# Local-attention layers: VectorE's mask and rows, ScalarE's table load, squares and copies in another order

## The reference, cut to what matters

```python
def attn_layer(x, Wqkv, qs, ksc, Wo):
    q, k, v = (sh(t) for t in jnp.split(x @ Wqkv, 3, -1))   # 16 heads of 64
    q, k = l2norm(q) * qs, l2norm(k) * ksc
    q = q * cos * scale + rotate_half(q) * sin * scale
    k = k * cos / scale + rotate_half(k) * sin / scale
    return local_attention(q, k, v) @ Wo                    # windows of 32, softmax over 64 keys

def ffn_layer(x, g, bln, W1, b1, W2, b2):
    a, gate = jnp.split(layernorm(x, g, bln) @ W1 + b1, 2, -1)
    return a * gelu(gate) @ W2 + b2

for i in range(6):
    x = attn_layer(shift_tokens(x), ...) + x
    x = ffn_layer(shift_tokens(x), ...) + x
```

## Time and profile before

| | |
|---|---|
| three runs | 2000.18, 2004.35, 2007.57 us, median 2004.35 |
| profiled execution, own time | 1996.81 us |
| its span | 1995.0 us |
| mean granted TensorE clock | 0.967 |
| first key projection of `local_layers` | 373.04 us into the span |
| end of its last step | about 1972 us |

### The profile page before, as it was taken

One profiled execution on the slowest core, in us unless ns is written; L12 is line 12 of the kernel. 1 busy time (PEld: TensorE's weight loads), 2 busy tenths in 40 slices (PEclk: granted clock), 3 DMA queues, 4 the chain that ended last, 5 costly groups with the idle time before them and its releaser, 6 DMA issues. The chain is left out here.

```text
span 1995.0 us, 59622 instructions
## 1 busy us (share of the span) xinstructions
PE 1797.9 (90%) x24192; PEld 1002.1 (50%) x24192; DVE 1538.6 (77%) x2549; ACT 1374.7 (69%) x2874; POOL 1262.5 (63%) x1127
## 2 busy tenths in 40 slices
PE   5898898679999999999999999999999999999974
PEld 3444444355555555555555555555555555555541
DVE  4778887357888888887888888888888888887833
ACT  1454445447878877787778887788877887778832
POOL 4303210248877877777777877778777787777710
PEclk8899999889999999999999999999999999999986
DMA  8000000323433333333443333333334333333300
GB/s 177 21 2 1 2 2 2 85 51 79 107 70 73 88 84 83 72 71 73 89 88 77 70 73 87 88 81 71 73 80 90 86 70 70 72 68 80 76 1 22
DMA packets 137216, 132.63 MB, mean 66 GB/s; under 512 B 79336, under 2 KB 82984, under 8 KB 136616
## 3 DMA queue, kind: packets, MB, share of 16 engines
q1 hardware_dynamic: 136944, 128.81, 29.1%
HBM read 20.94 MB, written 1.05 MB: 11 GB/s over the span
## 5 line engine op out<-in xcount | busy, mean ns | idle before, releaser
L1023 ACT ACTIVATE prob<-s_in,lower,rq 128x64 f32<-128x64 f32 x1536 | 542.9, 431 | 31.4 <-POOL lower L1193 31.1
L827 PE MATMUL bank_a<-x_shift,wqk_sb 128*128 128x512 f32 x768 | 369.4, 604 | 3.2 <-PEq L65 1.8
L1164 POOL TENSOR_TENSOR prob<-prob,rden 128x1024 f32<-128x1024 f32 x96 | 182.6, 1902 | 146.4 <-DVE rden L1244 146.3
L827 PEld LDWEIGHTS bank_a<-x_shift,wqk_sb 128*128 128x128 f32 x768 | 146.8, 195 | 183.0 <-issue 178.8
L1183 POOL TENSOR_TENSOR kfin<-rk,kfin 128x512 f32<-128x512 f32 x96 | 122.2, 1273 | 155.6 <-ACT rk L1119 107.1
L1009 ACT ACTIVATE zT<-bank_z 128x1024 f32<-128x1024 f32 x192 | 191.9, 1012 | 22.7 <-PE bank_z L838 22.7
L384 ACT ACTIVATE a_prob<-a_sT 128x1024 f32<-128x1024 f32 x128 | 130.5, 1023 | 103.5 <-PE a_sT L218 101.5
L493 DVE TENSOR_REDUCE a_negmax<-a_max 128x1 f32<-128x512 f32 x256 | 164.7, 685 | 47.8 <-PE a_max L168 44.2
L846 PE MATMUL bank_y<-zT,wvo_high 128*128 128x512 f32 x384 | 186.8, 609 | 0.9 <-ACT zT L1009 0.9
L846 PE MATMUL bank_y<-zT,wvo_low 128*128 128x512 f32 x384 | 186.1, 607 | 1.0 <-ACT zT L1009 1.0
L838 PE MATMUL bank_z<-pT,xk_prev 32*128 32x128 f32 x3072 | 167.1, 286 | 9.7 <-DVE xn L1266 5.2
(11 more groups left out here) (176 smaller groups left out, 4120.2 us busy)
## 6 DMA issues: line engine op xcount, KB each, us to landing
kpad<-kfin SPq DMA_DIRECT2D x384, 128.0 KB, 2.4
qpair<-qfin SPq DMA_DIRECT2D x384, 128.0 KB, 2.4
wqk_sb<-in_wqkv SPq DMA_DIRECT2D x40, 128.0 KB, 2.7
xk_prev<-xk_own SPq DMA_DIRECT2D x24, 192.0 KB, 2.6
ffn_sb<-in_ffn SPq DMA_DIRECT2D x6, 537.5 KB, 4.2
wvo_low<-in_wqkv SPq DMA_DIRECT2D x6, 256.0 KB, 5.7
wvo_low<-in_wo SPq DMA_DIRECT2D x3, 512.0 KB, 6.9
wvo_high<-in_wqkv SPq DMA_DIRECT2D x6, 256.0 KB, 4.8
```

What stands on the lines that cost most here:

```text
L827: last = pe.matmul(bank_a[:, half, :], wqk_sb[:, layer_of(u) % 2, part, half, g * P:(g + 1) * P], cols(u), start=True, stop=True)
L1023: last = act.activation(prob[:, n % 2, i, :], s_in[:, n % 2, i, :], ACT.Exp, bias=lower[:, n % 2, i:i + 1], scale=rq[:, n % 2, i:i + 1])
L1164: pool.tensor_tensor(prob[:, e % 2], prob[:, e % 2], rden[:].unsqueeze(2).broadcast_to([P, TPB * GH, 2 * WIN]), ALU.mult).then_inc(pn_ok, 1)
```

## The change

ScalarE, gelu step: the load of the ln and exp table stands between the key squares; ten exponentials follow it instead of nine; one more comes after the key norms; rq comes ahead of the first query square; both copies stand between the two query squares; exponentials 11 to 14 close the step, and number 15 opens the next one, under the same semaphore. ScalarE, other steps: the copy of banks 2 and 3 comes ahead of the second query square, and xnT behind exponentials 6 to 11. VectorE: mask and floor come ahead of xn; the pieces of ADD and OUTPUT stand at other places of the listing.

```diff
@@ scalar, step @@
+                if quarter(e) and unit_at(s - 1, LINEAR) is not None:
+                    exponentials(e, 15, TPB * GH).then_inc(exp_ok, 1)
                 if u_gelu is not None:
...
                         act.activation(sq[:, 0, :], bank_a[:, 0, :], ACT.Square).then_inc(sqk0_ok, 1)
+                    act.preload_act_table_set("natural_log_exp_and_others")
+                    if quarter(n):
                         after(act, pk2_ok, n)
                         act.activation(sq[:, 1, :], bank_a[:, 1, :], ACT.Square).then_inc(sqk_ok, 1)
-                    act.preload_act_table_set("natural_log_exp_and_others")
...
-                        exponentials(d, 0, 9)
+                        exponentials(d, 0, 10)
...
-                        after(act, q_mm, n)
-                        after(act, sumk_ok, n)
-                        act.activation(sq[:, 0, :], bank_a[:, 0, :], ACT.Square).then_inc(sqq0_ok, 1)
+                    if quarter(d):
+                        exponentials(d, 10, 11)
                     if quarter(c):
...
                     if quarter(n):
-                        after(act, pq2_ok, n)
-                        act.activation(sq[:, 1, :], bank_a[:, 1, :], ACT.Square).then_inc(sqq_ok, 1)
-                    if quarter(d):
-                        exponentials(d, 9, 11)
+                        after(act, q_mm, n)
+                        after(act, sumk_ok, n)
+                        act.activation(sq[:, 0, :], bank_a[:, 0, :], ACT.Square).then_inc(sqq0_ok, 1)
...
                         copy(z[:, 0:2, :], bank_z[:, 0:2, :]).then_inc(z01_ok, 1)
+                    if quarter(n):
+                        after(act, pq2_ok, n)
+                        act.activation(sq[:, 1, :], bank_a[:, 1, :], ACT.Square).then_inc(sqq_ok, 1)
                     if quarter(d):
-                        exponentials(d, 11, 16).then_inc(exp_ok, 1)
+                        exponentials(d, 11, 15)
                 else:
...
+                    if quarter(d):
+                        exponentials(d, 6, 12)
                     u_turned = unit_at(c, NORM)
...
-                    if quarter(d):
-                        exponentials(d, 6, 12)
...
-                    if quarter(n):
-                        after(act, pq2_ok, n)
-                        act.activation(sq[:, 1, :], bank_a[:, 1, :], ACT.Square).then_inc(sqq_ok, 1)
                     if quarter(e):
...
                         copy(z[:, 2:4, :], bank_z[:, 2:4, :]).then_inc(z23_ok, 1)
+                    if quarter(n):
+                        after(act, pq2_ok, n)
+                        act.activation(sq[:, 1, :], bank_a[:, 1, :], ACT.Square).then_inc(sqq_ok, 1)
@@ vector, step @@
-                if u_back is not None:
-                    after(dve, rstd_ok, u_back)
-                    after(dve, xnT_mm, u_back - 1)
-                    for t in range(TPB):
-                        last = dve.tensor_scalar(xn[:, t, :], ...)
-                    last.then_inc(xn_ok, 1)
                 if quarter(c):
...                                                    (mask)
                     dve.tensor_scalar(rk[:], bank_f[:], 1e-24, None, ALU.max).then_inc(floor_ok, 1)
+                if u_back is not None:
+                    after(dve, rstd_ok, u_back)
+                    after(dve, xnT_mm, u_back - 1)
+                    for t in range(TPB):
+                        last = dve.tensor_scalar(xn[:, t, :], ...)
+                    last.then_inc(xn_ok, 1)
+                if quarter(n):
...                                                    (query products, maxima)
+                if u_add is not None:                  (ADD, moved ahead of the folds and SUM)
+                    after(dve, y_mm, 4 * u_add + 3)
...
-                if u_add is not None:
...
+                if u_out is not None:                  (OUTPUT, moved ahead of LINEAR)
+                    after(dve, ff_mm, u_out)
...
-                if u_out is not None:
```

More of the change, by code:

```diff
@@ L1261, in step @@
                                   prob[:, e % 2].rearrange("p h (k n) -> p h k n", n=WIN)).then_inc(pT_ok, 1)
-                if u_back is not None:
-                    after(dve, rstd_ok, u_back)
-                    after(dve, xnT_mm, u_back - 1)
-                    for t in range(TPB):
-                        last = dve.tensor_scalar(xn[:, t, :], bank_z[:, 2, t * P:(t + 1) * P], mv[:, t, 0:1],
-                                                 rstd[:, t:t + 1], ALU.subtract, ALU.mult)
-                    last.then_inc(xn_ok, 1)
                 if quarter(c):
@@ L1279, in step @@
                     dve.tensor_scalar(rk[:], bank_f[:], 1e-24, None, ALU.max).then_inc(floor_ok, 1)
+                if u_back is not None:
+                    after(dve, rstd_ok, u_back)
+                    after(dve, xnT_mm, u_back - 1)
+                    for t in range(TPB):
+                        last = dve.tensor_scalar(xn[:, t, :], bank_z[:, 2, t * P:(t + 1) * P], mv[:, t, 0:1],
+                                                 rstd[:, t:t + 1], ALU.subtract, ALU.mult)
+                    last.then_inc(xn_ok, 1)
+                if quarter(n):
                     after(dve, q_mm, n)
@@ L1288, in step @@
                     dve.tensor_reduce(s_max[:], s_in[:, c % 2], AX.X, ALU.max, negate=True).then_inc(max_ok, 1)
+                if u_add is not None:
+                    after(dve, y_mm, 4 * u_add + 3)
+                    lo, hi = cols(u_add, 0, 64), cols(u_add, 64, P, 1)
+                    dve.tensor_tensor(lo, bank_y[0:64, :], lo, ALU.add)
+                    dve.tensor_tensor(hi, bank_y[64:P, :], hi, ALU.add).then_inc(xa_ok, 1)
                 if s < FOLD_STEPS:
@@ L1301, in step @@
                     last.then_inc(mv_ok, 1)
-                if u_add is not None:
[L1303 to L1306, removed]
+                if u_out is not None:
+                    after(dve, ff_mm, u_out)
+                    lo, hi = cols(u_out, 0, 64), cols(u_out, 64, P, 1)
+                    dve.scalar_tensor_tensor(lo, bank_z[0:64, 3, :], ff_column(u_out, 2 * FCH)[0:64], lo, ALU.add, ALU.add)
+                    dve.scalar_tensor_tensor(hi, bank_z[64:P, 3, :], ff_column(u_out, 2 * FCH)[64:P], hi, ALU.add,
+                                             ALU.add).then_inc(xf_ok, 1)
                 if u_lin is not None:
```

## The result

The changed kernel took 1992.75 us in the median of four runs (1990.03 to 1994.42), the kernel before 2003.21 (2000.18 to 2007.57, four runs): ratio 0.9945, interval 0.9923 to 0.9967. A second comparison, with six runs against thirteen, gave 0.9945 again (0.9924 to 0.9967). The forecast was 1993.0. That this number was met so closely is luck; it hides two errors that cancel: the steady steps gave 6 us, not 12, and 4 to 5 us net came from stalls that the forecast had not looked at.

What follows compares the result with a forecast made beforehand. TensorE was taken as the bound. Four steps of 61.88 against 62.47 us gave 0.57 a unit, 12.5 for 22, cut to 11.4 for early steps and stalls: 1993.0 from the median 2004.35, range 1984 to 2001.

Steps and rivals of the forecast that it cites:

- L838 ... must now wait ... 0.37 lost: Norm step: L838 overwrites the bank xn reads, so it waits for the later xn, costing TensorE 0.37 us.
- sumq then ends ... 2.48 into the gate step: GpSimd's queue moves forward by 0.53 us, so sumq ends 2.48 us into the gate step, against 3.15.
- The gelus at 1.29: Gelu step: ScalarE does not follow the shorter gate step, so gelus start 1.29 us in, before at 0.80.
- L940 starts at 6.91: Gelu step: the later second key square and sumk make L940 start at 6.91 us, before 6.58; cost 0.32.
- the third rival: Gelu steps: an unseen drain behind the table load delays L940 by 1.38 us each; slower, 2023 us; chance 0.02.
- The fourth: The square ahead of the last four exponentials delays exp_ok by 0.5 in three of four steps; say 2018 us; chance 0.05.
- The first: The xn wait doesn't bind and the gelu step's late gelus are absorbed: 21 us gained, 1984 us; chance 0.10.
- the fifth: No change at all, the gains below the noise: 2002 us; chance 0.08.
- the latency after L838: Sum and norm steps: 0.04 us assumed from a matmul's end to its reader on ScalarE or VectorE.
- the three heads (L846) want it at 1.72: a loss of 0.07: Gate step: the copy of banks 0 and 1 ends 1.74 us in, delaying the heads by 0.07.
- I count 0.1 a step, 0.7 us: Seven early steps without feed-forward work: the later copy of banks 0 and 1 costs 0.1 a step, 0.7 us.
- Rival 2: ScalarE becomes the carrier in gate and gelu steps; gelus 0.3 later still, half the gain lost, 1998 us; chance 0.26.

Runs made afterwards that it cites:

- e1: The kernel before with only VectorE's part of the change (mask and floor ahead of xn): 1991.02 us, ratio to before 0.9946.
- e3: The changed kernel with the second query square put back ahead of the copy of banks 2 and 3 outside gelu steps: 1978.92 us, ratio to before 0.9897.
- e6: The kernel of e3 with one of xn's four tiles put between mask and floor: 1974.70 us, ratio to before 0.9857.
- e9: The changed kernel with the DMAs spreading the second half of the queries made to wait for sumq: 2002.87 us, ratio to before 0.9992.
- e4: The changed kernel with the ln and exp table load put back behind both key squares: 1984.66 us, ratio to before 0.9915.

## Why the prediction was right or wrong

**Right, by its steps.** "L838 ... must now wait ... 0.37 lost": 0.34 idle, 0.43 by the starts. "sumq then ends ... 2.48 into the gate step": 2.43. "L940 starts with no wait" in gate steps: so. The gelus at 1.29: 1.29. "L940 starts at 6.91": 6.92. L888 in the gelu step at 12.87: 12.90. The moved pieces of ADD and OUTPUT, exponential 15 and xnT changed nothing that shows. The load with no drain behind it: 0.60 us of square begins 0.01 after its end, so the third rival is out, and the drain of about 1380 ns that the Trainium skill, "ScalarE: Activation LUTs", section "What ACT_TABLE_LOAD costs", gives does not show here. The fourth, slower through the exponentials, is out too: the sums of the probabilities in norm steps start where they did, at 1.75. The first, faster by more, is out by L838's wait, and the fifth, no change, by the interval of the ratio.

**Mis-sized: the steps' sum.** Forecast 15.99, 15.04, 15.30, 15.55; measured 16.02, 15.11, 15.47, 15.58. The gain is 0.27 a unit, under half of the forecast, 5.9 us for 22 units. (The forecast's own steps, 61.88 against 62.47, differ by 0.59, 13.0 us for 22; it wrote 0.57 and 12.5.) Three terms failed. First, the latency after L838: I took 0.04 us from a matmul's end to its reader, and a copy that finds its engine idle starts 0.06 to 0.07 after the modelled end, and takes 1.02 to 1.03. That is 0.03 in the sum step (no gain at all) and with xn's own 1.36 the 0.07 in the norm step. Second, and larger, the gate step: "the three heads (L846) want it at 1.72: a loss of 0.07". The start is late by 0.05, but the group of six then takes 2.68 instead of 2.58 and the scores 1.47 instead of 1.41, and L940 starts at 6.81, not at 6.66. Not all of it comes from the late heads: in e1 and e3, where they start at 1.72, L940 starts at 6.68 and not at 6.59, for a reason that no run shows. The late heads cost the other 0.13 (gate steps of 15.47 against 15.34). The sign was in the trace of an early step with a wait at L846 (step 8, of the earlier trace rows), where L929 follows after 2.68 as well; I used for the wait alone. Third, "I count 0.1 a step, 0.7 us" for the early steps: steps 3, 4, 6, 7 and 8 take 66.9 to 67.2 us in the three profiles of before, 68.2 and 68.7 in the two of the changed kernel, 1.3 to 1.7 us more. In e6, without the swap, they take 67.2.

**Not seen: the stalls.** 2003.21 less 1992.75 is 10.5 us; 5.9 are steady steps. The rest is TensorE waiting less for its instructions, and running less at half clock behind such waits. By the profiles (three against two), steps 12 to 94 lie 11.5 and 3.4 us above their medians, 8 us in favour of the change; the first twelve steps take 201.1 and 203.6, 2.5 us against it. e1 shows which part brings it: VectorE's part alone has the whole measured gain, and leaves qfin done 0.7 us earlier, since the floor comes earlier; ScalarE's part alone leaves qfin late and has none. That the time of the spread is the cause rests on e9. The forecast named stalls only as something that blurs the sum, and took the profiled execution, 0.4% under the median, as a fair one.

**Rival 2**, part of the gain given back by a ScalarE that became the carrier, has the size of the steady gain, half, and not its cause: the gelus came at 1.29, as forecast, and not 0.3 later. What it says of the gelu step (e3, e4) was in the forecast's own sum already.

## What to carry to other kernels

A piece of work that fits in an engine's wait is free only ahead of the wait's end: in norm steps ScalarE waits 1.2 us for L838 ahead of the copy, and the second query square of 0.6 us costs nothing there (e3); behind the copy it delayed the heads of the next step and a table load at its end. When two changes both eat the same room (late gelus, early load), test them together and apart; each was free alone. And where the median lies above the profiled execution, look at several executions for what differs, before the steady part is blamed or praised.

## What the runs showed of the hardware

TensorE's long waits in the midst of 128 short matmuls end 1.2 to 1.6 us behind a packet of 16 KB on the instruction queue, which uses the DMA engines that move the data: so the fetch of instructions can come last. The longest such wait in the gate steps was 2.43 us, in step 9 of e9 it was 4.03. A late packet started 1.3 to 1.9 us behind the last data, and so the waits were 1.6 to 2.3 us where the data ended 4.5 to 4.8 into the step, 0.7 where they ended at 3.6 to 3.7; one wait on SyncE, with the data ending at 5.0, made them 2.2 to 2.4. The five steps' stalls went from 13.3, 13.2 and 5.8 us to 2.2 and 3.8, and back to 8.8. Why the size differs between executions of one kernel stays open.

In steps 12 to 94 of the three profiles of before and the two of the changed kernel, the granted clock fell to 0.50 for 3.4 or 6.8 us at 6 of the 11 waits of 1.6 to 2.3 us, and once at a wait of 1.13; at the four of 0.7 it stayed at 1.00. At 0.50 four key projections took 3.62 us instead of 1.88.

A short wait on a semaphore can cost TensorE more than its idle time: 0.05 of lateness at L846 became 0.13 at L940 (6.81 against 6.68); what in the queue does this, no run here shows.
